# A convolution and spectral-attention block on one Trainium2 core: GpSimd normalises the convolution's result, an unused mean goes, and the order tables are rewritten

## The chip, the core and the metric

The kernel runs on one core of a Trainium2 chip. Its engines work in parallel, each through its own list in a fixed order, and they meet at semaphores: TensorE (PE in the profile; its weight loads are PEld), VectorE (DVE), ScalarE (ACT), GpSimd (POOL) and SyncE (SP), which here only issues DMAs. The metric is the device time of one execution in microseconds (us); smaller is better.

## The reference, cut to what matters

`x` has 32 images of 96 channels by 56 x 56 pixels, float32. Layer 0 is a depthwise 7 x 7 convolution, a layer norm over the channels, a two-layer perceptron (96, 384, 96) with exact GELU and a residual. Layer 1 is a spectral block and a second perceptron in 8-bit floats, each behind a layer norm over the channels:

```python
h = conv7x7_depthwise(x) + conv_b                       # layer 0
h = (h - mean(h)) * rsqrt(var(h) + 1e-5) * ln_g + ln_b
x = x + layer_scale * (gelu(h @ w1 + b1) @ w2 + b2)
t = tokens(x)                                           # (32, 3136, 96)
...
h = relu(bn1(_ln_t(t) @ aw1))
X = fft(h, axis=1)
X = relu(re(X)*rd - im(X)*idg + rb) + 1j * relu(im(X)*rd + re(X)*idg + ib)
t = t + bn2(ifft(X).real @ aw2)
...
t = t + ffn_fp8(_ln_t(t))
```

## The kernel before

**Two phases.** `conv_phase` makes the convolution for groups of four channels and stores it to DRAM in token layout (`h_dram`). `image_phase` does all the rest, image by image. A *turn* of its loop works on up to four images at once: part 1 (perceptron of layer 0, first layer norm of layer 1, forward transform, first half) on image n, part 2 (second half of the transform, the spectral step, first half of the inverse) on image n-1, part 3 (the inverse's rest and the 8-bit perceptron) on image n-2, and part "next" (layer norm of layer 0) on image n+1. Two turns fill the pipeline, turns n = 2 to 30 run as a loop (29 turns, kind "steady"), and others drain it.

**Steps.** A part is cut into steps, and a step into chunks c = 0 to 6 (0 to 7 in part 2); T2(0) below is chunk 0 of step T2. A chunk is 448 tokens (4 tiles of 112). Named by what PE does: M1, M2 are the two products of layer 0's perceptron; T turns its result for the statistics; W1 is `aw1`; A the outer transform; B the inner transform; W is `aw2`; IB and AP the inverse; S2 turns AP's result for the statistics, T2 turns the normalised tile back, F1, F2 are the 8-bit perceptron; HT turns the normalised convolution result. Steps without PE: L0S and L0N (statistics and normalisation of layer 0's norm), N2 (normalisation before F1), G (bias and relu between F1 and F2), FETCH (old residual from DRAM).

**Who does what around the norms.** VectorE makes statistics (`see`) and sums (`variances`), GpSimd raises them to the power -1/2 (`deviation`, L683), VectorE normalises (`normalize`, L831) with mean and deviation as per-partition scalars, PE turns the tile. The chain behind AP is: t2 (DVE, L903), S2 (PE), t_rows (ACT), see and variances (DVE), deviation (POOL), N2 (DVE), T2 (PE). The chain of part 2 is: B (PE), uw (ACT), plus and minus (DVE, L892), both (POOL, L712), W (PE), mixed (ACT), IB (PE).

**What sets the order.** Each engine's list comes from two tables written by hand: `STAGES` gives for each step the due index of chunk 0, the distance between chunks and their count; `LATER` shifts a step on one engine. `stages` sorts by the sum:

```python
steps = [(first + c * apart + later.get(name, 0), name, c) for part, wanted in parts.items() if wanted
         for name, (first, apart, count) in STAGES[part].items() for c in range(count)]
return [(name, c) for _, name, c in sorted(steps)]
```

The index is no time; an engine works through its list and waits where a semaphore isn't there yet. Psum banks are rings in PE's order: four for what ACT empties, two for what DVE empties (M2, T, W1, AP), two for B.

**Across two turns.** Step A stores the outer spectrum to DRAM chunk by chunk (three DMAs each, from SP's list). After A(6), SP waits for the stores and issues the load of `inner`: chunk 0 of B alone (336 KB), then all the rest (2016 KB and 42 KB). PE's B(0) of the next turn waits for the first, B(1) for the second. Behind these stand `out` (1176 KB), the load of `h` for the next image (1176 KB) and the fetches of `t_old` (168 KB each), all in one DMA queue. M1(0) of the next turn waits for ACT's `hn` of HT(6), L733.

Of the kernel before, what the change touches and what calls it, by code (L numbers as in the profile page):

```python
# [75 lines left out]
def before(n, k, per, ring):  # L76

    if k >= ring:
# [16 lines left out]
    "act": {"W": -0.5, "G": -0.5},  # L95
    "dve": {"B": 3, "M2": 2, "T": 2, "W1": 1, "F2": 2, "AP": 1, "S2": 1, "L0N": -1, "W": -2},
    "pool": {"B": 4, "T": 3, "S2": 2, "F1": 1},
    "sp": {"M2": 3},
# [325 lines left out]
def image_phase(nc, x_img, h_dram, t1_dram, g_dram, v_dram, wts, out_img):  # L424
# [8 lines left out]
    with ExitStack() as ctx:  # L433
# [372 lines left out]
        def _(dve):  # L806
# [19 lines left out]

            def normalize(which, c, dst, src, at):

                first = sums[which].shape[1] * (c % 2)
                for j in range(CH):  # L830
                    last = nc.vector.tensor_scalar(dst[:, j], src[:, j], sums[which][:, at + j, 3:4],  # L831
                                                   scales[which][:, first + at + j:first + at + j + 1],
                                                   ALU.subtract, ALU.mult)
                return last
# [500 lines left out]
```

## Time and profile before

| | |
|---|---|
| time, median of 3 runs | 4677.69 us (4676.67 to 4680.09) |
| the profiled execution | 4678.17 us, its span 4676.4 us |
| busy over the span | PE 85%, DVE 74%, ACT 49%, POOL 30% |
| one steady turn (25 of them take 3072.00 us) | 122.88 us |
| busy in one steady turn | PE 106.6, DVE 101.6, ACT 64.1, POOL 39.2 us |

The conv phase takes the first 0.65 ms. From there the profile repeats itself from turn to turn, so that one turn can be read for all. A stretch's busy times tell how much of each engine is used; the list of waits tells who waited for whom; the timeline shows each run of equal instructions with its start, its length, and in brackets the idle time ahead of it.

### The profile page before, as it was taken

To read this page: it belongs to the slowest core of one execution; us is meant where nothing else is said; L and a number is where in the kernel's file an instruction comes from. 1 tells how busy PE (TensorE), PEld (TensorE's weight loads), DVE (VectorE), ACT (ScalarE), POOL (GpSimd) and SP (SyncE) were. 2 spreads that over 40 slices of the span, in tenths; PEclk is the share of its full clock that TensorE was granted. 3 is DMA by queue.
4 is the path that set the end of the run, shared out by engine and by line. 5 is a ranking of instruction groups with operands and counts; after the bars stand their busy time and mean duration, and the time that the engine had idled before them with its cause. 6 is when DMAs were issued, how large, how long until landed. Compare 5 with 4: busy or idle time off the path is not lost.

```text
span 4676.4 us, 88192 instructions
## 1 busy us (share of the span) xinstructions
PE 3989.9 (85%) x22802; PEld 2808.8 (60%) x22802; DVE 3461.5 (74%) x11833; ACT 2285.2 (49%) x4610; POOL 1390.6 (30%) x1572
## 2 busy tenths in 40 slices
PE   5999969888888888888888888888888888888885
PEld 3444436666666666666666666666666666666664
DVE  2333346788888888888888888888888888888876
ACT  2444424455555555555555555555555555555543
POOL 1111233333332333333333333333333232333331
PEclk8999979999999999999999999999999999999986
DMA  6666524344444444444443333343444444444331
GB/s 172 166 169 172 163 71 107 94 111 115 111 113 113 111 112 115 109 113 115 110 114 105 98 102 107 102 108 105 108 113 114 111 113 114 112 112 113 100 91 49
DMA packets 420416, 532.48 MB, mean 114 GB/s; under 512 B 220047, under 2 KB 378493, under 8 KB 404413
## 3 DMA queue, kind: packets, MB, share of 16 engines
q1 hardware_dynamic: 405920, 510.40, 40.6%
q10 hardware_dynamic: 14272, 20.04, 1.7%
q14 instruction: 199, 1.63, 0.1%
q8 instruction: 25, 0.41, 0.0%
HBM read 295.18 MB, written 235.12 MB: 113 GB/s over the span
## 4 chain that ended last, share of the span: by engine, by line
PE 36%; DVE 30%; issue 12%; ACT 2%; POOL 2%; DVEq 1%; DMA 1%; ACTq 0%; POOLq 0%; SPq 0%
PE psum L993 9%; PE psum L987 7%; PE psum L1026 5%; DVE minus L892 5%; DVE xn L831 4%; DVE h_norm L831 4%; DVE plus L892 4%; DVE stats L809 3%; PE psum L1035 2%; PE psum L1007 2%; DVE act L875 2%; PE psum L1015 2%; PE psum L1049 2%; DVE h L922 1%; PE psum L1062 1%
## 5 line engine op out<-in xcount | busy, mean ns | idle before, releaser
L683 POOL TENSOR_TENSOR scales<-sums,minus_half 112x4 f32<-112x4 f32 (+1 forms) x480 | 636.6, 1355 | 2191.8 <-DVE sums L824 2191.8
L712 POOL TENSOR_TENSOR both<-plus,minus 96x224 f32<-96x224 f32 (+1 forms) x1024 | 618.2, 623 | 587.3 <-DVE minus L892 502.9
L993 PE MATMUL psum<-hid,w_sb 128*96 128x448 f32 x1344 | 592.8, 580 | 6.5 <-ACT hid L748 2.0
L987 PE MATMUL psum<-hn,w_sb 96*128 96x448 f32 x1344 | 557.2, 547 | 8.4 <-ACT h L796 6.9
L767 ACT ACTIVATE uw<-psum,spec 96x224 f32<-96x224 f32 (+1 forms) x1024 | 445.6, 511 | 157.5 <-PE psum L1026 154.9
L386 PE MATMUL c_psum<-c_xt,c_toeplitz 128*112 128x448 f32 x1152 | 476.6, 551 | 50.3 <-ACT c_xt L328 26.9
L414 DVE TENSOR_SCALAR c_h<-c_psum,c_bias 112x448 f32<-112x448 f32 x192 | 199.0, 1036 | 413.1 <-PE c_psum L386 413.1
L892 DVE SCALAR_TENSOR_TENSOR plus<-psum,spec,uw 96x224 f32<-96x224 f32 (+1 forms) x1024 | 426.8, 417 | 63.5 <-ACT uw L767 63.0
L748 ACT ACTIVATE hid<-psum,b_sb 128x448 f32<-128x448 f32 x672 | 419.7, 635 | 104.1 <-PE psum L987 61.9
L892 DVE SCALAR_TENSOR_TENSOR minus<-psum,spec,uw 96x224 f32<-96x224 f32 (+1 forms) x1024 | 425.8, 416 | 0.0
L1035 PE MATMUL psum<-aw_sb,both 96*112 96x96 f32 x3712 | 410.3, 263 | 4.7 <-ACT hid L748 4.7
L1026 PE MATMUL psum<-inner_dft,inner 112*96 112x112 f32 x3712 | 404.1, 261 | 4.8 <-DMA inner<-outer_spectrum 4.8
L1035 PEld LDWEIGHTS psum<-aw_sb,both 96*112 96x112 f32 x3712 | 395.3, 179 | 19.6 <-ACT hid L748 17.8
L1026 PEld LDWEIGHTS psum<-inner_dft,inner 112*96 112x96 f32 x3712 | 389.0, 165 | 23.1 <-issue 14.0
L875 DVE SCALAR_TENSOR_TENSOR act<-psum,scales,below 112x192 f32<-112x192 f32 x896 | 309.2, 406 | 96.4 <-PE psum L1007 88.6
L1062 PE MATMUL psum<-ident,xn 112*96 112x112 f32 x896 | 138.4, 282 | 278.8 <-DVE xn L831 278.8
L1007 PE MATMUL psum<-aw_sb,t 96*112 96x192 f32 x1792 | 343.6, 329 | 35.2 <-DVE t L853 35.1
L987 PEld LDWEIGHTS psum<-hn,w_sb 96*128 96x128 f32 x1344 | 246.2, 191 | 211.6 <-issue 154.8
L993 PEld LDWEIGHTS psum<-hid,w_sb 128*96 128x96 f32 x1344 | 218.5, 176 | 245.7 <-issue 220.6
L809 DVE BATCH_NORM_STATS2 stats<-t_rows 112x6 f32<-112x96 f32 x896 | 164.5, 246 | 253.6 <-ACT t_rows L781 253.6
L1007 PEld LDWEIGHTS psum<-aw_sb,t 96*112 96x112 f32 x1792 | 291.8, 177 | 95.4 <-DVE t L853 53.6
L1015 PE MATMUL psum<-act,outer_dft 113*114 113x192 f32 x1792 | 332.3, 328 | 19.1 <-DVE act L875 19.1
(85 smaller groups left out, 6549.5 us busy)
## 6 DMA issues: line engine op xcount, KB each, us to landing
outer_spectrum<-outer SPq DMA_DIRECT2D x448, 168.0 KB
inner<-outer_spectrum SPq DMA_DIRECT2D x32, 2016.0 KB
c_xpad<-x SPq DMA_DIRECT2D x96, 392.0 KB, 11.2
h_tokens<-c_h SPq DMA_DIRECT2D x24, 1568.0 KB, 8.4
h<-h_tokens SPq DMA_DIRECT2D x32, 1176.0 KB, 13.3
x_sb<-x SPq DMA_DIRECT2D x32, 1176.0 KB, 7.3
residual_stream<-t SPq DMA_DIRECT2D x224, 168.0 KB, 2.1
inner_inverse<-unmixed SPq DMA_DIRECT2D x224, 168.0 KB, 2.3
```

The lines of the kernel that those rows point to most:

```text
L386: last = pe.matmul(psum[0:PT, 4 + k % 4, 0:NB * NYB], toeplitz[:, c, half, BR * d:BR * (d + 1), :].rearrange("p t x -> p (t x)"), xt[:, sl ...
L683: nc.gpsimd.tensor_tensor(scales[which][:, at:at + w], su[:, :, 5], minus_half[:, 0:w], ALU.pow).then_inc(ready.sem, 1)
L712: last = nc.gpsimd.tensor_tensor(both[:, c % 2, m, 0:w, k * PT // 2:(k + 1) * PT // 2], half(plus), half(minus), ALU.subtract if k else AL ...
L748: nc.scalar.activation(hid[:, c % 2, m, :], bank("M1", c, m, CW, 128), ACT.Gelu, bias=b1_sb[:, m:m + 1]).then_inc(gelu_done.sem, 1)
L767: last = nc.scalar.activation(uw[:, j % 2, k, 0:w * PT // 2].rearrange("p (s k) -> p s k", s=w), re, ACT.Identity, bias=spec[:, m, shift:s ...
L892: last = nc.vector.scalar_tensor_tensor(out=dst[:, j % 2, k, 0:w * PT // 2].rearrange("p (s k) -> p s k", s=w), in0=im, scalar=spec[:, m, ...
L987: pe.matmul(bank("M1", c, m, CW, 128), w1_sb[:, m * 128:(m + 1) * 128], hn[:, c * CW:(c + 1) * CW], start=True, stop=True).then_inc(m1_mad ...
L993: last = pe.matmul(dst, w2_sb[:, m, :], hid[:, c % 2, m, :], start=(m == 0), stop=(m == KF - 1))
L1007: last = pe.matmul(dst[:, j * H2:(j + 1) * H2], t1[:, c % 4, at:at + PT], aw1_sb[:, :], start=True, stop=True)
L1015: last = pe.matmul(dst[:, j * H2:(j + 1) * H2], outer_dft[:, CH * c + 2 * m + j, :], act1[:, (2 * c + m) % 4, j, :], start=True, stop=True)
L1026: last = pe.matmul(dst[:, s * PT:(s + 1) * PT], inner[:, CH * c + s, m * C:(m + 1) * C], inner_dft[:, :], start=True, stop=True)
L1035: last = pe.matmul(dst[:, s * C:(s + 1) * C], both[:, c % 2, m, s, :], aw2_sb[:, m, :], start=(m == 0), stop=(m == 1))
```

## The change

Three things. (1) L0N's 28 `tensor_scalar` of a turn, 112 x 96 each, move from VectorE's list to GpSimd's; the mean's sign is turned for them in `variances`, so that GpSimd adds it. (2) For the norm whose weights are centred (`which == 1`), the mean is no longer computed: one small `tensor_scalar` less in each of 7 chunks. (3) `STAGES` and `LATER` have new numbers throughout.

```diff
-    1: {"M1": (-3, 11.8, NC), "M2": (7, 11.8, NC), "T": (13, 11.8, NC), "W1": (22, 11.8, NC), "A": (27, 11.8, NC)},
+    1: {"M1": (-0.5, 11.7, NC), "M2": (6.0, 11.8, NC), "T": (12.5, 11.7, NC), "W1": (22.0, 11.9, NC),
+        "A": (25.5, 12.7, NC)},
...
-    "next": {"L0S": (34, 3.4, NC), "L0N": (72, 3.3, NC), "HT": (79, 2.8, NC)},
+    "next": {"L0S": (35.5, 3.9, NC), "L0N": (94.5, 4.0, NC), "HT": (88.5, 3.0, NC)},
...
+    "pool": {"B": 6.5, "T": 5.0, "S2": 5.0, "L0N": -21.0, "L0S": -7.5},
+    "sp": {"M2": -2.0, "IB": -0.5, "A": 12.0, "FETCH": -8.0, "FETCH NEXT": 10.5},
...
+                    if name == "L0N":
+                        if c == 0:
+                            pool.wait_ge(ln0_ready.sem, ln0_ready.at(n + 1))
+
+                        b, j = before(n + 1, c, NC, 4)
+                        pool.wait_ge(ht_made.sem, ht_made.at(b, j))
+                        pool.sem_inc(passed, 1)
+                        for j in range(CH):
+                            q = CH * c + j
+                            last = nc.gpsimd.tensor_scalar(
+                                h_norm[:, c % 4, j, :].rearrange("p (k c) -> p k c", c=CC), h[:, :, q, :],
+                                sums[0][:, q, 3:4], scales[0][:, q:q + 1], ALU.add, ALU.mult)
+                        last.then_inc(h_normed.sem, 1)
...
+                if which != 1:
+                    nc.vector.tensor_scalar(su[:, :, 3], su[:, :, 0], 0.5 if which else -0.5, None, ALU.mult)
                 nc.vector.scalar_tensor_tensor(out=su[:, :, 4], in0=su[:, :, 2], scalar=C / 4.0, in1=su[:, :, 2],
-                                               op0=ALU.mult, op1=ALU.mult)
-                nc.vector.tensor_scalar(su[:, :, 3], su[:, :, 0], 0.5, None, ALU.mult).then_inc(step.sem, 1)
+                                               op0=ALU.mult, op1=ALU.mult).then_inc(step.sem, 1)
...
-                    if name == "L0N":
...
-                        normalize(0, 0, h_norm[:, c % 4, :, :].rearrange("p q (k c) -> p q k c", c=CC),
-                                  h[:, :, part, :].rearrange("p k q c -> p q k c"), CH * c).then_inc(h_normed.sem, 1)
```

Three places show what the new numbers do to the lists. The changed kernel's lines are two to fifteen higher for the same step (L980 is L982 there, L1062 is L1064, L712 is L726, and so on).

The first is PE near the start of a steady turn, before: S2(0), L1056, stands just ahead of the first row; the rows are M1(1), B(0) in two halves, T(0), AP(1) and T2(0).

```order
L987 MATMUL psum<-hn,w_sb 128x448
L971 REGISTER_ALU
L987 MATMUL psum<-hn,w_sb 128x448 x2
L1021 ISA
L971 ISA
L1026 MATMUL psum<-inner_dft,inner 96x112 x4
L971 REGISTER_ALU
L1026 MATMUL psum<-inner_dft,inner 96x112 x4
L997 REGISTER_ALU
L999 MATMUL psum<-ident,t 112x96 x4
L1049 MATMUL psum<-outer_inv,back 96x112 x4
L1062 MATMUL psum<-ident,xn 96x112 x4
```

The same place in the changed kernel: S2(0), B(0) and M1(1) stand ahead of the first row; the rows are T(0), AP(1), B(1) in two halves, S2(1) and T2(0).

```order
L1001 MATMUL psum<-ident,t 112x96 x4
L1051 MATMUL psum<-outer_inv,back 96x112 x4
L1023 ISA
L973 REGISTER_ALU
L1028 MATMUL psum<-inner_dft,inner 96x112 x4
L973 REGISTER_ALU
L1028 MATMUL psum<-inner_dft,inner 96x112 x4
L1056 REGISTER_ALU
L1058 MATMUL psum<-ident,t 112x96 x4
L973 REGISTER_ALU
L1064 MATMUL psum<-ident,xn 96x112 x4
```

T2(0) has moved behind B(1) and S2(1); B(1), which stood behind T2(0), M2(1) and S2(1), comes right after AP(1).

The second is PE at the end of a steady turn, before: F1(6), W1(6), HT(5) and HT(6), A(6) in two halves, F2(6), and then M1(0) of the next turn.

```order
L1070 MATMUL psum<-xq,fw_q 128x448 x3
L1007 MATMUL psum<-aw_sb,t 112x192 x4
L976 REGISTER_ALU
L980 MATMUL psum<-ident,h_norm 96x112 x4
L976 REGISTER_ALU
L971 REGISTER_ALU
L980 MATMUL psum<-ident,h_norm 96x112 x4
L1012 REGISTER_ALU
L971 REGISTER_ALU
L1015 MATMUL psum<-act,outer_dft 114x192 x2
L1012 REGISTER_ALU
L971 REGISTER_ALU
```

In the changed kernel the last rows of the turn are HT(4), A(6) in two halves, HT(5), F2(6) and HT(6).

```order
L982 MATMUL psum<-ident,h_norm 96x112 x4
L1014 REGISTER_ALU
L973 REGISTER_ALU
L1017 MATMUL psum<-act,outer_dft 114x192 x2
L1014 REGISTER_ALU
L1017 MATMUL psum<-act,outer_dft 114x192 x2
L978 REGISTER_ALU
L982 MATMUL psum<-ident,h_norm 96x112 x4
L1079 MATMUL psum<-hq,fw_q 96x448 x3
L978 REGISTER_ALU
L982 MATMUL psum<-ident,h_norm 96x112 x4
```

HT(5) and HT(6) have moved from ahead of A(6) to behind it, and HT(6) is now the last thing that PE does in a turn.

The third is GpSimd at the end of a steady turn, before: deviations of S2(6) and T(5), both of B(7), deviation of T(6).

```order
L683 TENSOR_TENSOR scales<-sums,minus_half 112x4
L697 REGISTER_ALU
L683 TENSOR_TENSOR scales<-sums,minus_half 112x4
L704 REGISTER_ALU
L707 REGISTER_ALU
L712 TENSOR_TENSOR both<-plus,minus 96x56 x2
L707 REGISTER_ALU
L712 TENSOR_TENSOR both<-plus,minus 96x56 x2
L692 REGISTER_ALU
L694 REGISTER_ALU
L683 TENSOR_TENSOR scales<-sums,minus_half 112x4
```

In the changed kernel: deviation of T(5), L0N(1), deviation of S2(6), L0N(2) and L0N(3), deviation of T(6), L0N(4), L0N(5), and then L0N(6).

```order
L684 TENSOR_TENSOR scales<-sums,minus_half 112x4
L701 TENSOR_SCALAR h_norm<-h,sums,scales 112x96 x4
L711 REGISTER_ALU
L684 TENSOR_TENSOR scales<-sums,minus_half 112x4
L697 REGISTER_ALU
L701 TENSOR_SCALAR h_norm<-h,sums,scales 112x96 x8
L708 REGISTER_ALU
L684 TENSOR_TENSOR scales<-sums,minus_half 112x4
L697 ISA
L701 TENSOR_SCALAR h_norm<-h,sums,scales 112x96 x4
L697 REGISTER_ALU
L701 TENSOR_SCALAR h_norm<-h,sums,scales 112x96 x4
```

The seven groups of four are new in GpSimd's list, with the last deviations between them; L0N(4) to L0N(6) stand behind the deviation of T(6).

## Rows read from the trace of the kernel before

**Rows 1.** The page, part 1: busy us, share of the span, instructions.

```profile
PE 3989.9 (85%) x22802; PEld 2808.8 (60%) x22802; DVE 3461.5 (74%) x11833; ACT 2285.2 (49%) x4610; POOL 1390.6 (30%) x1572
```

**Rows 2.** By stretch: PE, PEld, DVE, ACT, POOL busy us; clock; DMA share; GB/s.

```profile
1077.40:4149.40 3072.00, 2663.59 (x16351) 1950.90 (x16351) 2539.72 (x9075) 1602.05 (x3300) 979.69 (x1175) 0.99 0.41 109
2060.50:2183.40 122.90, 106.57 (x655) 78.09 (x655) 101.58 (x363) 64.12 (x133) 39.16 (x47) 0.99 0.41 109
2075.50:2079.50 4.00, 3.79 (x9) 2.02 (x10) 2.01 (x11) 0.54 (x1) 1.01 (x1) 0.57 1.02 352
```

**Rows 3.** PE's waits in 25 turns: us in total, times, longest.

```profile
PE psum L1062 <- DVE xn L831: 203.4, 75, 4.3
PE psum L999 <- DVE act L875: 81.1, 50, 2.0
PE psum L1056 <- DVE t L903: 33.1, 25, 1.3
```

**Rows 4.** Timeline of PE over a turn's start: start us, us, instructions.

```profile
2057.29 1.55 PE L1015 MATMUL psum<-act,outer_dft 113*114 113x192 f32 x8 [0.65 <-DVE act L875]
2059.70 0.74 PE L1077 MATMUL psum<-hq,fw_q 128*96 128x448 fp8e5 x3 [0.85 <-issue]
2060.47 2.49 PE L987 MATMUL psum<-hn,w_sb 96*128 96x448 f32 x6
...
2066.02 0.50 PE L1056 MATMUL psum<-ident,t 96*112 96x96 f32 x4
...
2070.50 0.93 PE L1049 MATMUL psum<-outer_inv,back 115*96 115x112 f32 x8
2075.71 0.95 PE L1062 MATMUL psum<-ident,xn 112*96 112x112 f32 x4 [4.27 <-DVE xn L831]
2076.45 3.75 PE L993 MATMUL psum<-hid,w_sb 128*96 128x448 f32 x6
...
2080.37 1.70 PE L1026 MATMUL psum<-inner_dft,inner 112*96 112x112 f32 x16
```

**Rows 5.** VectorE's groups by shape in 25 turns: busy us, mean ns of one, idle.

```profile
L831 DVE TENSOR_SCALAR h_norm<-h,sums,scales 112x96 f32<-112x96 f32 x700 | 178.0, 324 | 0.0
L822 DVE TENSOR_SCALAR sums<-sums 112x4 f32<-112x4 f32 x350 | 57.8, 165 | 0.0
```

**Rows 6.** GpSimd's groups by shape in the whole run.

```profile
L712 POOL TENSOR_TENSOR both<-plus,minus 96x224 f32<-96x224 f32 x896 | 581.6, 668 | 581.6 <-DVE minus L892 502.9 <-issue 73.1
...
L1234 POOL TENSOR_TENSOR scale<-scale,bn_row 96x96 f32<-96x96 f32 x1 | 0.4, 382 | 0.1
...
L1234 POOL TENSOR_SCALAR scale<-bn_row 96x96 f32<-96x96 f32 x1 | 0.3, 267 | 0.1
```

**Rows 7.** Timelines: two N2 chunks on VectorE, and GpSimd beside the second.

```profile
2141.53 1.05 DVE L831 TENSOR_SCALAR xn<-t_rows,sums,scales 112x96 f32<-112x96 f32 x4
...
2196.53 1.90 DVE L831 TENSOR_SCALAR xn<-t_rows,sums,scales 112x96 f32<-112x96 f32 x4
...
2196.79 1.33 POOL L712 TENSOR_TENSOR both<-plus,minus 96x224 f32<-96x224 f32 x2 [0.16 <-DVE minus L892]
```

**Rows 8.** Timeline of SP's DMA issues behind A(6).

```profile
2064.03 0.87 SPq L646 DMA_DIRECT2D inner<-outer_spectrum  x2
2064.95 4.75 SPq L647 DMA_DIRECT2D inner<-outer_spectrum  x1
...
2071.01 0.34 SPq L605 DMA_DIRECT2D h<-h_tokens  x1
```

**Rows 9.** The view of rows 2 for ten us of inner's load.

```profile
2065.50:2075.50 10.00, 5.94 (x40) 4.22 (x38) 7.06 (x23) 4.19 (x8) 3.60 (x5) 1.00 1.10 262
```

**Rows 10.** Timeline of ACT at a turn's end.

```profile
2054.04 0.72 ACT L733 ACTIVATE hn<-psum,ln_gb 96x448 f32<-96x448 f32 x1
...
2058.88 0.48 ACT L756 COPY outer<-psum 114x384 f32<-114x384 f32 x1 [0.17 <-PE psum L1015]
```

More of the change, by code:

```diff
@@ L84 @@
 STAGES = {
-    1: {"M1": (-3, 11.8, NC), "M2": (7, 11.8, NC), "T": (13, 11.8, NC), "W1": (22, 11.8, NC), "A": (27, 11.8, NC)},
-    2: {"B": (11, 9.3, ND), "W": (24, 9.3, ND), "IB": (28, 8.8, ND)},
-    3: {"AP": (3, 11.5, NC), "S2": (8, 11.5, NC), "N2": (14, 11.5, NC), "T2": (18, 11.5, NC), "F1": (20.5, 12, NC),
-        "G": (25, 11.5, NC), "F2": (32, 11.5, NC)},
-    "next": {"L0S": (34, 3.4, NC), "L0N": (72, 3.3, NC), "HT": (79, 2.8, NC)},
-    "fetch": {"FETCH": (9, 11.5, NC - 3)},
-    "fetch next": {"FETCH NEXT": (78, 1, 3)},
+    1: {"M1": (-0.5, 11.7, NC), "M2": (6.0, 11.8, NC), "T": (12.5, 11.7, NC), "W1": (22.0, 11.9, NC),
+        "A": (25.5, 12.7, NC)},
+    2: {"B": (8.0, 8.7, ND), "W": (18.0, 9.9, ND), "IB": (27.5, 8.9, ND)},
+    3: {"AP": (2.0, 11.1, NC), "S2": (6.5, 11.0, NC), "N2": (12.5, 11.4, NC), "T2": (17.5, 10.8, NC),
+        "F1": (21.0, 12.0, NC), "G": (23.5, 11.8, NC), "F2": (31.0, 12.1, NC)},
+    "next": {"L0S": (35.5, 3.9, NC), "L0N": (94.5, 4.0, NC), "HT": (88.5, 3.0, NC)},
+    "fetch": {"FETCH": (28.5, 10.5, NC - 3)},
+    "fetch next": {"FETCH NEXT": (103.0, 1.4, 3)},
 }
 LATER = {
[L95 to L98, printed above, removed]
[4 rows of a table added]
     "pe": {},
@@ L825, in variances @@
                                                op0=ALU.add, op1=ALU.add).then_inc(seen.sem, 1)
[L827 to L834, printed above, removed]
             def turn(kind, n):
@@ L916, in turn @@
                         dve.wait_ge(xt2_made.sem, xt2_made.at(*before(n, c, NC, 2)))
-                        normalize(2, c, xn2[:, c % 2, :, :], t2_rows[:, c % 2, :, :], 0).then_inc(xn2_done.sem, 1)
+                        for j in range(CH):
+                            at = CH * (c % 2) + j
+                            last = nc.vector.tensor_scalar(xn2[:, c % 2, j, :], t2_rows[:, c % 2, j, :], sums[2][:, j, 3:4],
+                                                           scales[2][:, at:at + 1], ALU.subtract, ALU.mult)
+                        last.then_inc(xn2_done.sem, 1)
                     if name == "G":
@@ L950, in turn @@
                             variances(0, n + 1, 0, LN0_EPS, ln0_seen)
-                    if name == "L0N":
-                        if c == 0:
-                            dve.wait_ge(ln0_ready.sem, ln0_ready.at(n + 1))
-                        b, j = before(n + 1, c, NC, 4)
-                        dve.wait_ge(ht_made.sem, ht_made.at(b, j))
-                        normalize(0, 0, h_norm[:, c % 4, :, :].rearrange("p q (k c) -> p q k c", c=CC),
-                                  h[:, :, part, :].rearrange("p k q c -> p q k c"), CH * c).then_inc(h_normed.sem, 1)
             turns(dve, turn)
```

2 rows, old and new, of the table LATER are left out of this document.

## The prediction

> **What bounds it now.** First the page: PE is busy 85% of the span and VectorE 74%, nothing else is near [rows 1]. These are means over fill and drain; the view by stretch gives the turn that is repeated. Twenty-five steady turns take 3072.00 us, 122.88 each, with PE busy 106.6 us and VectorE 101.6 us in each, ACT 64 and GpSimd 39 [rows 2]. So no engine fills the turn: PE idles 16.3 us of it, and the question is on whom it waits. The list of PE's waits answers: in 25 turns 203.4 us before T2 (L1062), three times a turn and 4.3 us at the longest, all for VectorE's N2; then 81.1 us before T (L999) for a psum bank that W1's VectorE step frees; 33.1 us before S2 (L1056) for VectorE's t2 [rows 3]. PE's bound is its own work plus waits for a VectorE that comes late, because VectorE itself is 83% full and works in an order that puts other steps ahead of the one waited for.
>
> The worst place is T2(0). PE ends AP(1) at 2071.43 and starts T2(0) 4.27 us later, for N2 [rows 4]. And that gap costs twice: in the four us around 2077 the granted clock is 0.57, a stretch at the lower level (1.2 GHz), where the steady mean is 0.99 [rows 2]; T2(0) takes 0.95 us and M2(1) 3.75 us there [rows 4]. An M2 at full clock I take to be as long as the M1 of the same size, 2.49 us [rows 4], and T2 at 0.55 (half clock, so a little over half of 0.95). The low clock thus adds 1.26 + 0.4, about 1.7 us a turn, which stands among "busy". PE's work at full clock is 106.6 - 1.7 = 104.9 us.
>
> **VectorE loses.** 700 normalisations take 178.0 us in 25 turns, 7.1 us a turn; of the 14 small L822 (165 ns each) seven go, and since their neighbours overlap them I count 0.1 us each, 0.7 us [rows 5] (bounds: nothing, and 7 x 0.165 = 1.2). That is 7.8 us less: 93.8 us of VectorE work beside 104.9 of PE's. VectorE's share of PE's work falls from 95% to 89%.
>
> **GpSimd gains.** 28 `tensor_scalar` of 112 x 96 with two scalars from SBUF. No such instruction is in the trace. Below: the one with immediate scalars, 96 elements a partition in 267 ns. Above: 668 ns, a `tensor_tensor` of 224 elements. Nearest: the `tensor_tensor` of 96 elements, 382 ns, since it too reads more than one operand [rows 6]. I take 0.38 us: 10.6 us a turn (7.5 to 18.7), 50 of a turn's 110 or more us. The time itself is hidden: GpSimd is idle over half the turn. What counts is who stands behind: four of them (1.5 us) come ahead of the deviation of S2(6), on which N2(6) and T2(6) wait, and L0N(4) to L0N(6) stand behind the deviation of T(6) and have HT(4) to HT(6), then M1(0), waiting for them. At 0.38 a chunk is ready about when PE comes to it, and late by a few us at 0.67; what that is worth is settled below, by a transfer that PE waits for anyway.
>
> **The port.** N2's four take 1.05 us alone and 1.90 us when GpSimd's `both` run beside them [rows 7]: the two engines hold each other up. The Trainium skill ("SBUF — State Buffer", section "Who interferes with whom") says why: a VectorE instruction in a two-port mode, or with two SBUF inputs, and a GpSimd instruction share one pair of ports, and whichever starts first keeps it to its end; the trace agrees, with 0.85 us lost on four instructions. L0N's 28 fall among G, N2 and F2 steps of VectorE, which are of that kind. Nothing lost would need that they never meet; all 10.6 us lost would need that VectorE always has such a step at hand. I put it in the leftover below with 1 us, and the heavy case among the rivals.
>
> **The order at T2(0).** B(1) and S2(1) now stand between AP(1) and T2(0). S2(0) starts at 2066.02 and T2(0) at 2075.71, 9.7 us later, of which 4.27 is waiting [rows 4]. The new order gives it M1(1), B(0), T(0), AP(1), B(1), S2(1) in between: the old 5.4 us plus B(1), 1.70, and S2(1), 0.5, so 7.6 us, and on VectorE N2(0) has only what it had ahead of it. N2(0) itself is done sooner than today, because VectorE's S2(0) and B(0) directly follow each other; I expect the 4.27 us gone and with it the low clock. The two other T2 waits (203.4/25 - 4.27 = 3.9 us) get more PE work between S2 and T2 the same way.
>
> **A new wait at B(1).** B(1) moves the other way, to the front, and A(6) to the back, and between these two lies a transfer. Today A(6) ends on PE at 2058.84; ACT's second copy of it ends at 2059.36 [rows 10]; the stores, their landing, and SP issues `inner` at 2064.03 [rows 8]. The three loads, 2394 KB or 2.45 MB, at the 262 GB/s of that stretch take 9.4 us from 2065.5 [rows 9], so all has landed at about 2074.9, 16.0 us after A(6). B(1) starts at 2080.37 [rows 4], 5.5 us after that: hidden today. In the new order PE has between A(6) and B(1): HT(5), F2(6), HT(6), M1(0), AP(0), M2(0), S2(0), B(0), M1(1), T(0), AP(1). The eight from M1(0) on are the same that run today without a wait from 2060.47 to 2071.43, 10.96 us; F2 is 0.74 and I take 0.4 for each HT, by S2's 0.5 less overlap [rows 4]. M1(0) now also waits for ACT's `hn` of HT(6), 0.72 plus 0.2 us of hand-over [rows 10], since nothing stands between: 0.9 us. Sum 1.5 + 0.9 + 10.96 = 13.4 us. And A(6)'s copy comes some 0.4 us later on ACT, behind three HT copies of 0.72. So B(1) waits 16.0 + 0.4 - 13.4 = 3.0 us, every turn. As this segment is now set by the transfer, lateness of HT(5), HT(6) up to 3 us costs nothing, which is why GpSimd's price matters little up to 0.67. The two fetches of `t_old` that now stand behind `inner` in the queue land some 0.7 us each after it, and AP(1)'s add waits for the first; S2(1), which needs that, stands behind B(1)'s 1.7 us. The load of `h` stands behind all of these and `out` in the one queue: 5.2 MB in all, which at 262 GB/s from 2065.5 has landed some 26 us after A(6). VectorE's L0S(0), which needs it, has moved forward; between AP(1) and it stand T(0), B(1), M2(1), S2(1), W1(0), G(0) and N2(1). 93.8 us for 71 VectorE steps a turn are 1.3 each, so from B(1)'s 16.4 on these take 9 to 10 us and L0S(0) comes up at about 26 as well: a wait of a us or none, left to the leftover.
>
> **The leftover.** Today's idle time apart from T2's is 16.3 - 8.1 = 8.2 us. With VectorE lighter a quarter of that stays, 2.1, to which T2 adds little; with the port's 1 us less what the B(1) wait absorbs I take 2.3 us. This is chosen; its bounds are 0 and 8.2.
>
> **Sum.** 104.9 + 0.9 (M1(0)) + 3.0 (B(1)) + 2.3 = 111.1 us a turn, 11.8 less than 122.88. Over the 29 turns of the loop 342 us. The first drained turn, nearly the same work, gives some 8 us more (an estimate, two thirds of 11.8); in the first filling turn, where L0N lies on the path, 28 x (0.38 - 0.25) = 4 us are lost. Against the profiled execution's 4678.17 us (span 4676.4; 0.5 us over the median of the runs): 4678.2 - 342 - 4 = 4332 us.
>
> **Rivals.** *The leftover is nil* (chance 0.15): VectorE at 89% keeps up everywhere, 108.8 us a turn, 4265 us. For it: today's VectorE is dense only where L0N stood; against: two-bank rings tie the two engines step by step.
> *The port takes back half* (0.22): VectorE is held through half of L0N's 10.6 us and passes that on to PE, 116.4 us a turn, 4486 us. For it [rows 7]; against: `both` runs today for 18 us a turn (581.6 us over 32 images), nearly twice what L0N will, and VectorE lives with it [rows 6].
> *Slower* (0.06): GpSimd's price is so high that HT(6) is late. Behind the deviation of T(6) stand 12 instructions; up to 0.67 us each they hide behind the transfer, from there 0.1 us more costs 1.2 us a turn, so the gain of 11.8 is gone at 1.65 us each. At 2 us the turn is 127 us, 4796 us in all. Against it: no plain arithmetic of this size is near that on GpSimd [rows 6].
> *Nothing happens* (0.03): PE's waits only change places, 4678 us. The list of waits speaks against it, as all the long ones are for VectorE, which loses 7.8 us.
> The forecast keeps 0.54.
>
> **Chances and range.** A measurement of this kernel can tell about 0.2%, 9 us, from no change. Faster: 0.54 + 0.15 + 0.22 = 0.91; the same 0.02; slower 0.07. The range 4235 to 4490 us is 107.8 to 116.5 us a turn; it holds the forecast, half of the first rival and beyond its centre, and most of the second, some 0.8.
>
> **What would show it.** Right: a turn of 109 to 113 us; no wait of 4 us before T2, and no stretch at half clock behind it; a wait of 2 to 4 us before B (L1028) for the DMA of `inner`, once a turn; `h_norm` on GpSimd at 0.27 to 0.67 us; VectorE busy 94 to 97 us a turn. Wrong: `h_norm` above 1 us; N2, G or F2 on VectorE much longer than today; PE waiting for HT; a wait at B(1) as long as today's at T2(0), with the lower clock behind it; VectorE waiting for `h` at L0S(0).

## The result, and the profile after

The changed kernel takes 4497.26 us (median of 4 runs, 4495.98 to 4501.97), the kernel before in the same comparison 4678.77 us: a ratio of 0.961 (95% interval 0.960 to 0.963). It is 181 us faster where 346 us had been forecast, and 7 us above the upper end of the range.

The page's part 1 of the changed kernel, which answers to [rows 1], and then the view by stretch, which answers to [rows 2]: 27 steady turns in one stretch, one turn, and two short stretches inside that turn.

```profile
PE 4006.1 (89%) x22802; PEld 2904.3 (65%) x22802; DVE 3307.4 (74%) x10713; ACT 2254.2 (50%) x4610; POOL 1840.4 (41%) x2468
```

```profile
1000.00:4150.00 3150.00, 2890.46 (x17641) 2191.47 (x17640) 2616.17 (x8849) 1702.94 (x3562) 1446.96 (x2025) 0.96 0.43 115
1775.88:1892.97 117.09, 106.29 (x654) 80.78 (x655) 96.98 (x328) 63.07 (x132) 52.90 (x75) 0.97 0.44 115
1791.10:1794.40 3.30, 3.30 (x20) 3.30 (x19) 3.19 (x14) 1.92 (x4) 1.01 (x1) 0.50 1.05 277
1883.20:1886.50 3.30, 3.30 (x13) 2.69 (x11) 0.61 (x2) 2.29 (x5) 1.64 (x4) 0.50 0.49 101
```

A turn now takes 116.7 us on average (it varies from 114.6 to 118.1, where before it was always within 0.2 us of 122.9). PE is busy 107.1 us of it, about as long as before (106.6), and idles 9.6 us instead of 16.3. What the reader should see is the clock column: 0.96 where [rows 2] had 0.99. There are now two places in this turn at half clock, not one. The stretches at the lower level add up to 9.0 us a turn, before to 3.4.

PE's waits in the stretch of 27 turns, which answer to [rows 3] (us in total, times, longest):

```profile
PE psum L982 <- ACT outer L770: 81.9, 24, 3.7
PE psum L1028 <- DMA inner<-outer_spectrum: 69.0, 26, 3.8
PE psum L1009 <- DVE t L859: 39.8, 54, 1.7
PE psum L989 <- ACT hn L747: 26.6, 27, 1.0
PE psum L982 <- POOL h_norm L701: 23.6, 24, 3.3
...
PE psum L1064 <- DVE xn L925: 5.7, 25, 0.3
```

Divided by 27: the wait before T2 (L1064), 8.1 us a turn before, is 0.2 us. At B(1) (L1028) stands the forecast wait for `inner`, 2.6 us, and at M1(0) (L989) the one for `hn`, 1.0 us. The longest in total is one that the prediction doesn't have: PE at HT (L982), 3.0 us a turn, for ACT's copy of the outer transform. The timeline of PE at the turn's start (of [rows 4]) shows B(1)'s wait and what follows it:

```profile
1785.92 0.93 PE L1051 MATMUL psum<-outer_inv,back 115*96 115x112 f32 x8
1790.34 2.65 PE L1028 MATMUL psum<-inner_dft,inner 112*96 112x112 f32 x16 [3.49 <-DMA inner<-outer_spectrum]
...
1793.43 0.95 PE L1064 MATMUL psum<-ident,xn 112*96 112x112 f32 x4
```

B(1) takes 2.65 us where it took 1.70, and T2(0) its 0.95 again [rows 4]: the wait moved from T2 to B(1), and the half clock moved with it. The second place is the unforeseen wait, at the turn's end. Timeline of SP's issues, ACT and PE there:

```profile
1873.11 0.33 SPq L614 DMA_DIRECT2D residual_stream<-t  x1
1873.62 0.33 SPq L595 DMA_DIRECT2D x_sb<-x  x1
1874.06 1.45 SPq L637 DMA_DIRECT2D outer_spectrum<-outer  x3
...
1877.18 1.47 PE L1017 MATMUL psum<-act,outer_dft 113*114 113x192 f32 x8
...
1882.21 0.86 ACT L770 COPY outer<-psum 114x384 f32<-114x384 f32 x2 [3.11 <-DMA outer_spectrum<-outer]
1882.84 0.61 PE L982 MATMUL psum<-ident,h_norm 112*96 112x112 f32 x4 [3.44 <-ACT outer L770]
```

This is a chain of three queues. SP issues M2(6)'s store, the load of `x_sb` (1176 KB, 7.7 us to landing) and only then the three stores of A(3), all into one DMA queue. `outer` in SBUF has two buffers, so ACT can't copy A(5) out of psum before A(3)'s stores are done; ACT's ring has four banks, so PE's HT(1) can't start before ACT has copied A(5). HT(1) and everything behind it come 3.44 us late, and W1(6) and F1(6) then run at half clock. The place comes from the numbers in the diff: on SP, A(3) sorts at 25.5 + 3 x 12.7 + 12.0 = 75.6, and M2(6), which issues `x_sb`'s load as well, at 6.0 + 6 x 11.8 - 2.0 = 74.8. In the old tables A(3) and A(4) stood ahead of M2(6).

Last, L0N's group on GpSimd in the same stretch, which answers to [rows 6]; the second fence holds the spread of its instruction in the whole run (least, median, most, in ns).

```profile
L701 POOL TENSOR_SCALAR h_norm<-h,sums,scales 112x96 f32<-112x96 f32 x756 | 397.9, 542 | 94.8 <-PE psum L982 94.7
```

```profile
L701 POOL TENSOR_SCALAR h_norm<-h,sums,scales x896: 413/426/1217, 657.5 to 4226.7; 112x96 f32<-112x96 f32 x180
```

On VectorE it is N2's instruction, `xn`, that takes longer. Its group in 25 turns of the kernel before, in the stretch of the changed kernel, and in the same stretch of e4 (below), which has the new order with L0N on VectorE:

```profile
L831 DVE TENSOR_SCALAR xn<-t_rows,sums,scales 112x96 f32<-112x96 f32 x700 | 203.7, 353 | 1.9
```

```profile
L925 DVE TENSOR_SCALAR xn<-t_rows,sums,scales 112x96 f32<-112x96 f32 x756 | 285.2, 438 | 19.8 <-POOL scales L684 19.8
```

```profile
L912 DVE TENSOR_SCALAR xn<-t_rows,sums,scales 112x96 f32<-112x96 f32 x750 | 260.3, 407 | 0.0
```

### The profile page after: what moved, and what is told of

It is laid out like the page before. It is cut to its first block, busy times and chain, and to the rows that moved or that the text cites. A ratio compares the mean times of both kernels' runs of the same rounds, so it can differ in the third digit from the quotient of the medians.

```text
span 4494.2 us, 88363 instructions
## 1 busy us (share of the span) xinstructions
PE 4006.1 (89%) x22802; PEld 2904.3 (65%) x22802; DVE 3307.4 (74%) x10713; ACT 2254.2 (50%) x4610; POOL 1840.4 (41%) x2468
## 4 chain that ended last, share of the span: by engine, by line
PE 29%; DVE 26%; DMA 13%; issue 10%; ACT 3%; SPq 2%; POOL 1%; DVEq 1%; ACTq 0%; POOLq 0%
DMA inner<-outer_spectrum 6%; PE psum L989 6%; DMA outer_spectrum<-outer 6%; DVE stats L823 5%; PE psum L1009 5%; PE psum L1028 4%; PE psum L995 4%; DVE minus L898 4%; DVE plus L898 3%; DVE t L859 3%; PE psum L1037 2%; DVE h L932 2%; DVE xn L925 2%; PE psum L1017 2%; DVE act L881 2%
## 5 line engine op out<-in xcount | busy, mean ns | idle before, releaser
L684 POOL TENSOR_TENSOR scales<-sums,minus_half 112x4 f32<-112x4 f32 (+1 forms) x480 | 605.8, 1266 | 1686.2 <-DVE sums L839 1685.7
L726 POOL TENSOR_TENSOR both<-plus,minus 96x224 f32<-96x224 f32 (+1 forms) x1024 | 642.7, 653 | 356.6 <-DVE minus L898 297.8
L989 PE MATMUL psum<-hn,w_sb 96*128 96x448 f32 x1344 | 566.3, 559 | 31.8 <-ACT hn L747 31.8
L995 PE MATMUL psum<-hid,w_sb 128*96 128x448 f32 x1344 | 554.7, 549 | 2.1 <-ACT hid L762 2.0
L1028 PE MATMUL psum<-inner_dft,inner 112*96 112x112 f32 x3712 | 431.2, 271 | 90.5 <-DMA inner<-outer_spectrum 89.8
L701 POOL TENSOR_SCALAR h_norm<-h,sums,scales 112x96 f32<-112x96 f32 x896 | 461.3, 531 | 103.2 <-PE psum L982 102.9
L1028 PEld LDWEIGHTS psum<-inner_dft,inner 112*96 112x96 f32 x3712 | 406.0, 173 | 110.9 <-issue 86.4
L1009 PE MATMUL psum<-aw_sb,t 96*112 96x192 f32 x1792 | 374.2, 353 | 46.5 <-DVE t L859 46.5
L989 PEld LDWEIGHTS psum<-hn,w_sb 96*128 96x128 f32 x1344 | 248.9, 195 | 215.1 <-issue 192.6
L1009 PEld LDWEIGHTS psum<-aw_sb,t 96*112 96x112 f32 x1792 | 320.1, 191 | 94.0 <-DVE t L859 62.7
L790 ACT COPY mixed<-psum 112x384 f32<-112x384 f32 (+1 forms) x256 | 114.6, 448 | 470.8 <-PE psum L1037 470.8
L925 DVE TENSOR_SCALAR xn<-t_rows,sums,scales 112x96 f32<-112x96 f32 x896 | 332.9, 432 | 23.5 <-POOL scales L684 23.5
```

The source lines that it names most:

```text
L684: nc.gpsimd.tensor_tensor(scales[which][:, at:at + w], su[:, :, 5], minus_half[:, 0:w], ALU.pow).then_inc(ready.sem, 1)
L701: last = nc.gpsimd.tensor_scalar(h_norm[:, c % 4, j, :].rearrange("p (k c) -> p k c", c=CC), h[:, :, q, :], sums[0][:, q, 3:4], scales[0][ ...
L726: last = nc.gpsimd.tensor_tensor(both[:, c % 2, m, 0:w, k * PT // 2:(k + 1) * PT // 2], half(plus), half(minus), ALU.subtract if k else AL ...
L925: last = nc.vector.tensor_scalar(xn2[:, c % 2, j, :], t2_rows[:, c % 2, j, :], sums[2][:, j, 3:4], scales[2][:, at:at + 1], ALU.subtract, ...
L989: pe.matmul(bank("M1", c, m, CW, 128), w1_sb[:, m * 128:(m + 1) * 128], hn[:, c * CW:(c + 1) * CW], start=True, stop=True).then_inc(m1_mad ...
L995: last = pe.matmul(dst, w2_sb[:, m, :], hid[:, c % 2, m, :], start=(m == 0), stop=(m == KF - 1))
```

## One account for all kernels

So that runs can be compared, each turn is split in three. *Idle* is the turn less PE's busy time. *Clock* is half of the time that PE was busy in stretches whose granted clock was at the lower of the two levels. *Work* is the rest, PE's busy time as it would be at 2.4 GHz. All are means over 24 steady turns of the profiled execution; the times are medians. The kernel before stood at 4678 to 4680 us in all comparisons.

| kernel | time, us | turn | idle | clock | work |
|---|---|---|---|---|---|
| before | 4678.8 | 122.9 | 16.3 | 1.7 | 104.9 |
| changed | 4497.3 | 116.7 | 9.6 | 4.2 | 102.9 |
| e1 x_sb later | 4522.7 | 117.7 | 9.4 | 5.2 | 103.1 |
| e2 inner in three | 4514.3 | 117.7 | 10.0 | 4.7 | 102.9 |
| e3 both | 4551.0 | 118.9 | 10.4 | 5.4 | 103.1 |
| e4 L0N on VectorE | 4504.9 | 117.6 | 10.2 | 4.4 | 103.0 |
| e5 the move alone | 4949.5 | 132.7 | 19.5 | 8.9 | 104.3 |
| e6 stores earlier | 4439.9 | 115.2 | 7.6 | 4.7 | 102.9 |
| e7 x_sb by ScalarE | 4481.8 | 116.3 | 9.4 | 3.9 | 102.9 |
| e8 three edits | 4463.5 | 116.0 | 8.1 | 4.9 | 102.9 |
| e9 the mean alone | 4715.0 | 124.4 | 16.0 | 3.6 | 104.8 |
| e10 L0N sooner | 4449.4 | 115.2 | 8.7 | 3.7 | 102.7 |
| e11 four edits | 4394.3 | 113.7 | 7.3 | 3.8 | 102.6 |
| e12 four, on VectorE | 4378.4 | 113.8 | 8.2 | 1.7 | 103.9 |

The turn before less the turn after, 6.2 us by 29 turns, is 179 of the 181 us. It is made of 6.7 us less idle, 2.0 us less work, and 2.5 us more for the clock.

## The experiments

### e1 to e3: the two waits of the changed kernel

The first edit issues `x_sb`'s load behind A(3)'s stores instead of ahead of them; the second loads `inner` in three pieces, so that B(1) waits for chunk 1 alone; e3 has both.

```diff
 e1, SP                                    e2, SP and PE
-  if followed and c == NC - 1:            -  enumerate(((0, CH), (CH, NS - 1)))
-      load_x()                  # in M2   +  enumerate(((0, CH), (CH, 2 * CH), (2 * CH, NS - 1)))
+  if name == "A" and c == 3 and followed: -  if c < 2:
+      load_x()                            +  if c < 3:      # waits for its own piece
```

> The changed kernel, with only the load of x_sb issued later: behind the stores of A(3) in SP's list, no longer behind M2(6)'s store ahead of them. Theory (a transfer ahead of A(3)'s stores): ACT's step A(5) no longer waits for these stores, PE's 3.0 us wait before HT(1) goes, and with it one of the stretches at half clock; the turn falls from 116.7 to about 112.5 us, the time to 4360 to 4400 us. Rival (GpSimd and its port make the last third late anyway): the wait before HT only changes its releaser to h_norm, the time stays within 20 us of 4497.

> The changed kernel, with the load of inner cut in three instead of two, so that B(1) waits for chunk 1 alone (336 KB). Theory (B(1) waits for 2 MB that it doesn't need): PE's 2.6 us before B(1) go, and the half clock behind it; but AP(1)'s add still waits for t_old, so some 1 us of it comes back at S2(1); 2 to 3.5 us a turn, 4395 to 4440 us. Rival (VectorE is the pace by then): the gap moves behind B(1), less than 20 us gained.

> Both edits, the late load of x_sb and inner in three parts. Theory: two separate waits, so the gains add: about 110 us a turn, 4270 to 4330 us, and next to no half clock in a steady turn. Rival: either wait hides the same lateness, so that both together give hardly more than the better one alone.

All three missed what was expected and were slower than the changed kernel, e2 by little more than the spread of the runs: ratios to before of 0.967 (0.965 to 0.969), 0.964 (0.963 to 0.966) and 0.972 (0.970 to 0.973). Each removed its wait, and each time another stood there. PE's waits in e1, then e2, then e3, in the same stretch:

```profile
PE psum L1028 <- DMA inner<-outer_spectrum: 110.9, 43, 4.5
PE psum L982 <- POOL h_norm L701: 56.7, 49, 1.8
...
PE psum L982 <- ACT outer L770: 6.6, 27, 0.2
```

```profile
PE psum L1058 <- DVE t L909: 91.0, 26, 4.8
PE psum L982 <- ACT outer L770: 60.9, 18, 3.7
```

```profile
PE psum L1058 <- DVE t L909: 125.5, 26, 5.9
```

In e1 the wait at HT(1) fell from 81.9 to 6.6 us, so the chain above is right. But `x_sb`'s 1.2 MB then stood in the same queue ahead of the stores of IB(7), of `back` and of A(6), and `inner` was issued 10.4 us after A(6)'s end instead of 4.1 (in the turns read). Of the 75 us that the wait at HT(1) gave up, the wait for `inner` took 42 (69.0 to 110.9) and the wait of HT for GpSimd's `h_norm` 33 (23.6 to 56.7), and the clock came on top. In e2 the wait at B(1) went to S2(1) (L1058), which needs AP(1)'s add, which waits for `t_old`, which stands behind `inner` in the queue. This is the fetch that the prediction named, and it had been covered only by B(1)'s wait. The theory that the two waits are worth their length by themselves fell.

### e4, e5, e9: the parts of the change, alone

e4 keeps the new order and puts L0N back on VectorE, at the place in the list that it has on GpSimd. e5 keeps the old tables and moves only L0N to GpSimd, at the index that it had on VectorE; unlike the changed kernel, it subtracts the mean there instead of adding the mean with its sign turned. e9 keeps the old tables and drops only the mean; for the other two norms it is made one instruction sooner, as in the changed kernel.

```diff
 e4 (of the changed kernel; the step's code moves to the VectorE block)
-    "dve": {... "L0N": 0.5, ...}
+    "dve": {... "L0N": -21.0, ...}
 e5 (of the kernel before; the step's code moves to the GpSimd block)
-    "pool": {"B": 4, ...}
+    "pool": {"L0N": -1, "B": 4, ...}
+                                sums[0][:, q, 3:4], scales[0][:, q:q + 1], ALU.subtract, ALU.mult)
 e9 (of the kernel before)
+                if which != 1:
+                    nc.vector.tensor_scalar(su[:, :, 3], su[:, :, 0], 0.5, None, ALU.mult)
                 nc.vector.scalar_tensor_tensor(out=su[:, :, 4], in0=su[:, :, 2], scalar=C / 4.0, in1=su[:, :, 2],
-                                               op0=ALU.mult, op1=ALU.mult)
-                nc.vector.tensor_scalar(su[:, :, 3], su[:, :, 0], 0.5, None, ALU.mult).then_inc(step.sem, 1)
+                                               op0=ALU.mult, op1=ALU.mult).then_inc(step.sem, 1)
```

> The changed kernel with all its new order, but L0N on VectorE again, at the place in VectorE's list that corresponds to GpSimd's. Theory (the order alone brings part of the gain, VectorE's 7 us are needed for the rest): VectorE at 96% of PE's work again, 3 to 6 us a turn more than the changed kernel, 4580 to 4680 us. Rival (the port costs VectorE what it was spared): within 30 us of 4497, or faster.

> The kernel before, with its old order tables, and only L0N on GpSimd, at the same index in GpSimd's list as it had in VectorE's. Theory (the move alone is worth little, as PE waits for VectorE only some 4 us in the third of the turn in which L0N stood): 0 to 4 us a turn, 4560 to 4680 us. Rival (VectorE's 7 us are the gain, the order only tunes it): 6 us a turn or more, below 4510 us.

> The kernel before without the unused mean alone, all tables as they were. If the order of the work sets the turn (as the run with L0N put back on VectorE says), 7 small instructions less on VectorE give 0 to 10 us: 4668 to 4680. If VectorE's busy time sets it, 0.7 us a turn, some 20 us or more: 4650 to 4660.

e4: 0.963 (0.961 to 0.964), which overlaps the changed kernel's interval, as the rival had it. VectorE is busy 102.4 us a turn, more than before the change, and the turn is 117.6 us; yet the wait before T2 isn't in PE's list any more. So the new order, with the mean dropped, makes practically the whole gain. GpSimd's part in it is 8 us, which the two intervals don't tell from nothing.

```profile
1000.00:4150.00 3150.00, 2880.64 (x17513) 2174.43 (x17512) 2738.84 (x9527) 1692.62 (x3537) 1067.62 (x1256) 0.96 0.43 115
```

e5: 1.057 (1.055 to 1.059), 271 us slower than before, where both expectations had a gain or no change. The wait for VectorE's `xn` before T2 stays though VectorE is 5.6 us a turn lighter, and a new one for `h_norm` at HT stands beside it; below, PE's waits, and then GpSimd's group, in the stretch of e5:

```profile
PE psum L1067 <- DVE xn L844: 196.9, 71, 4.9
PE psum L985 <- POOL h_norm L700: 136.5, 87, 3.5
```

```profile
L700 POOL TENSOR_SCALAR h_norm<-h,sums,scales 112x96 f32<-112x96 f32 x657 | 551.9, 849 | 0.2
```

One instruction takes 849 ns on average here, and GpSimd runs it without idle time in between (0.2 us): PE waits at HT for L0N, 5.8 us a turn (the stretch holds 3150 / 132.7 = 23.7 turns). The turn gets 9.8 us longer: 3.2 more idle, 7.2 more for the clock, 0.6 less work.

But e5 isn't the change's move by itself, since its instruction is another one. The spread of it in e5, to be set against 413/426/1217 in the changed kernel:

```profile
L700 POOL TENSOR_SCALAR h_norm<-h,sums,scales x896: 675/681/2222, 658.0 to 4688.4; 112x96 f32<-112x96 f32 x180
```

None of the 896 takes less than 675 ns, where half of the changed kernel's take 426 or less. What runs beside them isn't the reason. In the turn that fills the pipeline the 28 of them run in one go while VectorE runs nothing; GpSimd's timeline there in e5, then in the changed kernel:

```profile
657.96 18.74 POOL L700 TENSOR_SCALAR h_norm<-h,sums,scales 112x96 f32<-112x96 f32 x28 [0.24 <-POOL scales L683]
```

```profile
657.54 11.35 POOL L701 TENSOR_SCALAR h_norm<-h,sums,scales 112x96 f32<-112x96 f32 x28 [0.24 <-POOL scales L684]
```

The two kernels' instructions differ in subtract against add alone, and that makes 18.74 us of 11.35: 0.26 us an instruction, 7.4 us of GpSimd's time a turn. This is what the turned sign in the change is worth, and e5 gave it away. What the move with the addition does in the old order was not run, so e5 says nothing certain about the move alone.

e9: 1.007 (1.005 to 1.009), 35 us slower for less work, which neither expectation had. Two turns of e9, and the same stretch of the kernel before:

```profile
1575.20:1697.98 122.78, 106.68 (x654) 77.94 (x654) 100.75 (x356) 64.08 (x132) 39.15 (x47) 0.99 0.41 110
1823.50:1951.22 127.72, 111.77 (x656) 81.67 (x655) 100.84 (x356) 64.18 (x132) 39.17 (x47) 0.93 0.40 105
```

```profile
1569.00:1691.81 122.81, 106.48 (x655) 78.02 (x654) 101.58 (x363) 64.09 (x132) 39.16 (x47) 0.99 0.41 110
```

The two turns of e9 run the same instructions, and PE idles 16.1 us in the first and 16.0 in the second (length less busy). Yet the second is 4.9 us longer, nearly all of it PE's busy time (5.1), at a clock of 0.93. PE's timeline at T2(1) in the first and in the second of them:

```profile
1608.94 0.56 PE L1063 MATMUL psum<-ident,xn 112*96 112x112 f32 x4 [2.60 <-DVE xn L832]
1609.33 1.70 PE L1027 MATMUL psum<-inner_dft,inner 112*96 112x112 f32 x16
...
1857.67 0.95 PE L1063 MATMUL psum<-ident,xn 112*96 112x112 f32 x4 [2.61 <-DVE xn L832]
1858.42 3.19 PE L1027 MATMUL psum<-inner_dft,inner 112*96 112x112 f32 x16
```

The same wait of 2.6 us stands ahead of both, and behind one of them T2 and B take nearly twice as long. In the kernel before, every turn draws one stretch at half clock, at the same place; in e9 some turns draw two or three. That is the loss: idle and work hardly change, the clock costs 1.9 us more a turn. Why one turn draws it and the next doesn't isn't settled here.

### e6, e7, e8: the queue again

e6 moves A's stores and the next turn's fetches one step forward on SP, so that A(3)'s stores come ahead of M2(6)'s store and `x_sb`; of the rest only A(2)'s stores change place, with the store of IB(4) behind them. e7 gives `x_sb`'s load to ScalarE's queue. e8 is e7 with `inner` in three and `t_old` fetched ahead of A(6)'s stores.

```diff
 e6
-    "sp": {"M2": -2.0, "IB": -0.5, "A": 12.0, "FETCH": -8.0, "FETCH NEXT": 10.5},
+    "sp": {"M2": -2.0, "IB": -0.5, "A": 11.0, "FETCH": -8.0, "FETCH NEXT": 9.5},
 e7 (in ACT's turn; load_x() in SP's M2 goes)
-    "act": {"F2": 0.5, ...}
+    "act": {"M2": 3.3, "F2": 0.5, ...}
+    if name == "M2" and c == NC - 1 and kind in ("first", "second", "steady"):
+        act.wait_ge(t1_done.sem, t1_done.at(n, c))
+        act.dma_start(x_sb[0:C, :], ...).then_inc(x_loaded.sem, 16)
 e8 = e7, the edit of e2, and
-    "FETCH NEXT": 10.5
+    "FETCH NEXT": 7.5
```

> The changed kernel with step A one index earlier in SP's list, so that A(3)'s stores are issued ahead of M2(6)'s store and of the load of x_sb; FETCH NEXT is shifted alike and keeps its place. Theory (one DMA queue, in which x_sb's 1.2 MB hold back whatever stands behind): the wait before HT(1) goes as in the run with the late load, but back and A(6)'s stores are not pushed back by it, since x_sb stays as early as it was; the time from A(6) to B(1) grows by 2 to 3 us because PE reaches A(6) earlier; 1 to 3 us a turn gained, 4410 to 4470 us. Rival (the half clock takes back what idle time goes): no gain, 4480 to 4530 us.

> The changed kernel with the load of x_sb issued from ScalarE's queue, after M2(6), so that it no longer stands in SP's queue ahead of the small stores. Theory (the queue): ACT's wait for A(3)'s stores and PE's before HT(1) go, back and inner come no later than in the changed kernel; about 112 to 114 us a turn, 4370 to 4440 us. Rival (the 16 DMA engines are the limit, whichever queue issues; or the half clock takes it back): 4480 us or more.

> The run before this one, and inner in three parts, and the fetches of t_old for the next turn's chunks 0 to 2 issued ahead of A(6)'s stores. Theory (all three waits at the turn's end are transfers): neither B(1) nor AP(1) waits, 110 to 112 us a turn, 4300 to 4380 us. Rival (the half clock): the granted clock's low stretches stay at 9 to 13 us a turn and the time at 4450 us or above.

e6: 0.949 (0.947 to 0.950), 57 us faster than the changed kernel and as expected: the wait at HT(1) is gone (6.6 us in 27 turns), and `x_sb` delays nobody. These are two numbers, each one smaller. The turn is 1.5 us shorter and not the 3.0 us of that wait: HT's wait for `h_norm` grew by 1.2 us a turn (23.6 to 56.7 us in the stretch), and the clock costs 0.5 more. What is left:

```profile
PE psum L1028 <- DMA inner<-outer_spectrum: 59.6, 27, 4.5
PE psum L982 <- POOL h_norm L701: 56.7, 46, 1.8
```

e7: 0.958 (0.956 to 0.959), 15 us faster than the changed kernel instead of 57 to 127. The timeline says why:

```profile
1870.67 0.37 ACTq L742 DMA_DIRECT2D x_sb<-x  x1
1871.11 1.45 SPq L635 DMA_DIRECT2D outer_spectrum<-outer  x3
...
1878.89 0.86 ACT L772 COPY outer<-psum 114x384 f32<-114x384 f32 x2 [2.22 <-DMA outer_spectrum<-outer]
```

`x_sb` goes out on ACT's queue and A(3)'s stores 0.4 us later on SP's, with only M2(6)'s store ahead of them, and ACT still waits for them until 1878.89: 7.8 us after their issue, where it was 8.2 in the changed kernel (1874.06 to 1882.21). M2(6)'s store itself, issued in the same moment as `x_sb`, takes 4.9 us to landing, where it took 2.0 in the changed kernel. So a second queue wasn't a second path here: the transfers share what carries them. The Trainium skill ("DMA: Bandwidth & Descriptors", section "Issuing engines are not separate DMA queues") says so, and this row agrees. e8: 0.954 (0.953 to 0.956): B(1) waits no more, but HT(1) does, and the clock costs 4.9 us, which is what its rival had.

### e10 to e12: putting the edits together

e10 is e6 with L0N sooner by 2 of the index on GpSimd, where L0N(4) waited behind the deviation of T(6). e11 adds `inner` in three and the `t_old` fetches ahead of A(6)'s stores. e12 is e11 with L0N on VectorE as in e4.

```diff
 e10 = e6 and
-    "pool": {..., "L0N": -21.0, "L0S": -7.5},
+    "pool": {..., "L0N": -23.0, "L0S": -7.5},
 e11 = e10, the edit of e2, and
-    "FETCH NEXT": 9.5
+    "FETCH NEXT": 6.5
 e12 = e11 and the edit of e4
```

> The run with the stores of A(3) earlier (4440), and L0N two steps sooner on GpSimd's list, so that L0N(4) stands ahead of the deviation of T(6), which it waited behind. HT(5) and HT(6) then don't wait for h_norm (2.1 us a turn in that run). Theory: all between A(6) and B(1) is set by the transfer of inner, 17 us from A(6)'s end, so B(1)'s wait takes the 2 us up and the time stays: 4420 to 4450, with the wait at B(1) at 4 to 5 us a turn. Rival: GpSimd's lateness and the half clock that follows it are worth their own 2 to 5 us a turn: 4300 to 4390.

> That kernel, with inner's load in three (B(1) waits for chunk 1 alone) and the fetches of t_old ahead of A(6)'s stores. Theory: the transfer of inner is then on nobody's path, and the waits at HT(1), B(1), S2(1) and before M1(0) go together, and most of the half clock with them: segments as short as the shortest seen in any run give 110 to 111 us a turn, 4290 to 4330. Rival: another wait or the half clock takes their place, as in the earlier runs with several edits: 4390 to 4440.

> The kernel with four edits, with L0N on VectorE instead of GpSimd. If the move to GpSimd is worth its 5.4 us of VectorE a turn once the transfer is off the path: slower than the run with four edits by 60 to 160 us. If the order alone makes the gain, as in the new order with L0N put back: within 20 us of it.

e10: 0.951 (0.949 to 0.952), no different from e6, as the theory had it: the wait for `h_norm` halves, and the one at B takes it up (120.3 us against 59.6), because from A(6) to B(1) the transfer sets the length.

```profile
PE psum L1028 <- DMA inner<-outer_spectrum: 120.3, 50, 4.4
...
PE psum L982 <- POOL h_norm L701: 27.8, 27, 1.0
```

e11: 0.939 (0.937 to 0.940), 46 us faster than e6, though 64 to 104 short of what was expected, and inside the rival's range. SP's issues show the new place of the wait:

```profile
1736.16 0.64 SPq L666 DMA_DIRECT2D back<-inner_inverse  x2
1736.91 1.39 SPq L637 DMA_DIRECT2D outer_spectrum<-outer  x3
1738.80 1.49 SPq L599 DMA_DIRECT2D t_old<-residual_stream  x3
1740.39 1.44 SPq L637 DMA_DIRECT2D outer_spectrum<-outer  x3
1746.94 1.40 SPq L647 DMA_DIRECT2D inner<-outer_spectrum  x3
```

`back` (1197 KB), A(5)'s stores and three fetches stand ahead of A(6)'s stores, and `inner` is issued 5.1 us after the last of these was, where the changed kernel needs 2.1 (issued until 1774.75, `inner` at 1776.84). B(0) waits instead of B(1).

e12 is the fastest kernel, 0.935 (0.933 to 0.936), 119 us under the changed kernel and 16 us under e11, with VectorE nearly 6 us a turn heavier (2827.74 us in this stretch against 2671.07 in e11). Its view by stretch and the first of its waits:

```profile
1000.00:4150.00 3150.00, 2922.10 (x18130) 2182.20 (x18129) 2827.74 (x9858) 1759.93 (x3658) 1127.60 (x1300) 0.99 0.44 119
```

```profile
PE psum L1007 <- DVE t L846: 52.7, 52, 1.9
...
PE psum L1026 <- DMA inner<-outer_spectrum: 33.8, 22, 2.0
```

No wait in its list is longer than 2.0 us, those for `h_norm` are 4.8 us in all, and the clock is back at 0.99. So L0N on GpSimd, worth nothing measurable in the changed order, costs a little in a better one (the two kernels' intervals don't meet). Where it costs isn't shown: in the profiled executions the steady turns are equally long (113.8 and 113.7 us), with 2.1 us less for the clock in e12 and as much more idle and work.

## Why the prediction missed

**What held.** The wait before T2 went, 8.1 to 0.2 us a turn. B(1) waits for `inner` once a turn, 2.6 us where the sum has 3.0; M1(0) waits 1.0 where it has 0.9. The price of GpSimd's instruction is 426 ns (median) where 380 was taken, 542 on average, inside the bounds; a subtraction would have cost 675 at least, outside them (e5). VectorE is busy 97.0 us a turn, not 93.8. Of the difference 2.4 us are the 28 `xn`, 438 ns each where they took 353. But L0N on GpSimd accounts for only 31 ns of the 85, 0.9 us a turn, since e4 has 407 without it; the rest came with the new order. That is about the 1 us that the prediction gave the port. The leftover, 2.3 in the sum, is 3.0: 1.5 at L1009, 0.9 for `h_norm`, 0.6 in two smaller waits. It was chosen and not derived, so that it comes near is luck.

**The first step that failed: moved past one queue, followed for one chunk.** The part on B(1) follows A(6)'s stores through SP's list and takes no account of A(3)'s, which the new numbers moved behind a load of 1.2 MB. The wait that follows, 3.0 us a turn at HT(1), is in no term of the sum. e6 shows it: A(3)'s stores moved back in front, and the wait is gone. PE waiting for HT was among the prediction's own signs of being wrong; it came, though more for ACT's copy of the outer transform (81.9 us in the stretch) than for GpSimd (23.6).

**The second, and the larger: "and with it the low clock".** The sum sets all of PE's work at full clock. It had [rows 2] before it, half clock behind a wait of 4.27 us, and itself put a wait of 3.0 us at B(1) at no such price. The clock cost 4.2 us a turn, 2.5 more than before; by 29 turns the 4.2 are 122 of the 165 us that are missing. In the account the forecast thus becomes 111.1 + 3.0 (HT(1)) + 4.2 (clock) + 0.7 (leftover) - 0.4 (B(1)) + 0.1 (M1(0)) - 2.0 (work) = 116.7 us, which is the turn measured. The last term has no cause that was tried here. It goes with the order, as all kernels with the new order have it (102.6 to 103.9 against 104.3 to 104.9); short waits inside a run of matmuls count as busy, which could be the reason.

**Half of the reason given fell too.** The prediction's first part gives two reasons for PE's waits: VectorE is 83% full, and its order puts other steps ahead of the one waited for. The leftover rests on a lighter VectorE. e4 gives VectorE all of L0N back, and neither the wait before T2 returns nor more than 8 us of the gain goes; e12, with VectorE 90% full (2827.74 of 3150 us), is the fastest of all. Which step stands ahead of which decided, and not how full the engine is. The rival that the port takes back half came out at the right time, 4486 us, for a wrong reason: in e4 no L0N on GpSimd can hold VectorE up, and it takes as long, with the same waits at HT(1) and B(1) (76.1 and 65.9 us in the stretch).

**Open.** What makes the same wait draw half clock in one turn and not in the next (e9), and so how much of a gain the clock gives back; part of the differences between e6, e7, e8 and e10 may be of this kind. The length of the wait doesn't settle it: in the kernel before, three waits of more than 2 us a turn stand before T2 and one half-clock stretch follows, and e12, without a wait over 2.0 us, still pays 1.7 us a turn. Two kernels were not run: the new order with the mean kept, and the old order with L0N added on GpSimd.

## What to carry to other kernels

When a table moves a step, look at every chunk of it in every queue, and ask which big transfer each small store now stands behind: here one step in SP's list was worth 57 us, more than the work moved between engines. Time the very operation on the engine that it moves to: a subtraction in place of an addition cost GpSimd 7.4 us a turn. Before moving work off a busy engine, ask whether PE waits for its load or for its order; putting the work back in the new order costs one run and answers it. Count a wait of a few microseconds on PE with the half clock that may follow, and expect a removed wait to show up at the next thing in the same queue.
